# A four-level Perceiver block: reordering inside the last cross attention, and turned logits in the soft mixture of experts

## The chip, the cores and the metric

The kernel runs on one core of one Trainium2 chip. The metric is the device time of one execution in microseconds (us), taken as the median of several executions. The engines are TensorE (PE: matrix products and transposes, its weight loads shown apart as PEld), VectorE (DVE), ScalarE (ACT), GpSimd (POOL) and the queue of the SyncE engine (SP), from which every transfer of this kernel is issued. All arithmetic around the change is in float32.

## The reference

The kernel computes twelve residual layers on `x` (2 batches, 128 tokens, width 256); a cross attention reads a context of 2048 tokens per batch. The change touches two of the twelve.

The soft mixture of experts of level 1 (16 experts, 128 slots each, hidden width 64):

```python
x_n = _l2norm(x_ln, -1) * scale
mu_n = _l2norm(mu, 0)
logits = jnp.einsum('bnd,des->bnes', x_n, mu_n)
dispatch = jax.nn.softmax(logits, axis=1)                            # over the 128 tokens
combine = jax.nn.softmax(logits.reshape(B, N, E * S), axis=-1)       # over the 2048 slots
slot_in = jnp.einsum('bnd,bnes->besd', x_ln, dispatch)
h = jax.nn.gelu(jnp.einsum('besd,edh->besh', slot_in, W1) + b1[None, :, None, :], approximate=False)
slot_out = jnp.einsum('besh,ehd->besd', h, W2) + b2[None, :, None, :]
out = jnp.einsum('bsd,bns->bnd', slot_out.reshape(B, E * S, D), combine)
```

The cross attention of level 3 (16 query heads of width 128, 4 key/value heads; the keys are the context and the 128 tokens themselves, 17 tiles of 128):

```python
q = _rope(_rms_norm((x @ Wq.T)...)); k = _rope(_rms_norm((kv_in @ Wk.T)...)); v = kv_in @ Wv.T
scores = jnp.einsum('bhqd,bhkd->bhqk', q, k) * SCALE
probs = jax.nn.softmax(scores, axis=-1)
attn = jnp.einsum('bhqk,bhkd->bhqd', probs, v)
return attn.transpose(...).reshape(...) @ Wo.T
```

## The kernel before

Each layer is a block: a hand-written program for each engine, tied by semaphores, with a barrier of all engines at its end. Order within an engine is the order in which the block's function issues. PSUM has eight banks of 128x512 float32.

**Soft mixture of experts (`l1_ffn`, L1217 to L1526).** `xst` is the normalised `x`, turned, `xlt` the layer-normed one, `k.mu` the slot matrix 256x2048, `k.mu_row` the reciprocal norms of its columns spread over all partitions, `k.mu_col` the same reciprocals laid down the partitions, one column per expert (made in `l1_attn`, L1141 to L1169). The logits are made twice:
- `combine_logits(n)` (L1289; its matmuls are recorded at the helper's L212): tokens on the partitions, 512 slots at a time, eight pieces, into banks 4, 5, 2 in turn (`PIECE_BANK`); `take_logits(n)` on DVE multiplies by `k.mu_row` into `comb` (L1465) and takes the maximum (L1467); `combine_exps(b)` on ACT (L1411) exponentiates all 2048 in place.
- `dispatch_logits(p)` (L1304, also recorded at L212), for each of eight pairs of experts: slots on the partitions, eight 128x256 matmuls into bank 0. `dispatch_max(p)` on DVE (L1476, L1477) finds the maximum over tokens, `exps(p)` on ACT (L1406) exponentiates with `k.mu_col` as scale.

Behind that, for each pair: `dispatch_norm` (DVE L1482, L1484), `turn` (PE L1320), `take_turned` (DVE L1490), `hidden` (PE L1344), `gelu` (ACT L1422), `slot_out` (PE L1355), `add_bias` (DVE L1505); `turn_combine` (PE L1332) turns the pair's part of `comb`, `take_combine` (DVE L1496) copies it, `combine` (PE L1363) adds up the output in banks 6 and 7. The pairs are software pipelined: iteration i issues on PE, in this order, `dispatch_logits(i)`, `turn(i-1)`, `turn_combine(i-3)`, `hidden(i-2)`, `slot_out(i-3)`, `combine(i-4)` (L1370). On ACT, iteration i is `exps(i)` and `gelu(i-2)`, which need different function tables, so that a table is loaded before each. `first_product(n)` (four pieces of `x_ln @ W1`, copied out by `take_product(n)` on ACT, L1416) and the eight `combine_logits` lie inside iterations 0 and 1.

**Cross attention (`l3_xattn`, L2196 to L2738).** The work is in eight units u (batch x key/value head, four query heads each). `loop(u)` in this text is the loop over the 17 key tiles j at L2484: PE issues `values(u, j)` (L2416, weighs the values with the exponentials of tile j), `scores(u+1, j)` (L2389), and at some j a `project(u+2, i)` (L212) or a `turn_group(u+2, i)` (L2379). A tile of 128x512 weights, `wt(j)`, lives through: scores in one of three PSUM banks; `copy_scores` (ACT L2557); `maxima` (DVE L2674, the first is a copy, L2671); later `shifts` (DVE L2684, subtracts the row's maximum), `exps` (ACT L2567), `values` (PE). `copy_scores(u+1, j)` waits until `values(u, j)` has read the tile. Between two loops stands `between(u)` on each engine: PE turns the maxima (`turn_max`, L2396, waits for the last `maxima`), spreads them (`spread_max`, L2402), and, for u of 2 and more, makes five value pieces (`project_values`, L212 with `x_wv`; units 0 and 1 make one, their others come from earlier layers), which ACT copies (`take_values`, L2542); `turn_out(u-1)` (L2425, copied by ACT at L2574) and `project_out(u-1)` (L212) finish the unit before.

How far the shifts and the exponentials run ahead of the loop:

```python
AHEAD_SHIFT, AHEAD_EXP = 3, 2                       # L2245
for j in range(AHEAD_SHIFT): shifts(u, j)           # DVE, L2719, then in the loop:
    if j + AHEAD_SHIFT < KT3: shifts(u, j + AHEAD_SHIFT)
    if u + 1 < NU: maxima(u + 1, j)
    if j + AHEAD_EXP < KT3: exps(u, j + AHEAD_EXP)  # ACT, L2622
    if u + 1 < NU: copy_scores(u + 1, j)
```

DVE has extra work in two loops: `angle_step` (L2151 to L2165) at j of 8 and more in loop(0), `table_step` (L2178 to L2185) at j of 12 and more in loop(1), and ACT has `sines` (L2193) ahead of loop(1). POOL finishes the projected keys and queries (L2505 to L2514).

## Time and profile before

| | us |
|---|---|
| median of 3 runs (range) | 1604.55 (1602.79 to 1605.17) |
| the profiled execution's own time | 1604.83 |
| span of its profile | 1603.1 |
| PE busy | 1413.8 (88%) |
| DVE busy | 1122.8 (70%) |
| ACT busy | 868.8 (54%) |
| POOL busy | 469.7 (29%) |

The profile records one execution. Its span runs from the first to the last instruction; the 1.7 us up to that execution's own time lie around it. A busy share is an average over all twelve layers; what a change is worth is read in its own layer. "PEclk" is TensorE's granted clock as a share of 2.4 GHz, so 0.50 is 1.2 GHz.

### The profile page before, as it was taken

The numbers are of one execution on the slowest core, as the hardware profiler recorded it, in microseconds if no ns is written. First come the engines' busy times: TensorE is split into PE (matmuls) and PEld (weight loads), VectorE is DVE, ScalarE is ACT, GpSimd is POOL, SyncE is SP. The second block draws the span as 40 slices with busy tenths as digits, with TensorE's granted clock in tenths as the row PEclk, the third lists the DMA queues.
The fourth block names the chain that finished last, engine by engine and source line by source line (L and its number), as shares of the span: only waits on it lengthen the run. The fifth ranks groups of instructions, "written<-read, shape, count | busy, mean of one in ns | idle before, by whom it ended". The sixth has DMA issues, their size and how long they took to land. (4 is left out here: it accounts for less than half of the span.)

```text
span 1603.1 us, 23976 instructions
## 1 busy us (share of the span) xinstructions
PE 1413.8 (88%) x8072; PEld 993.9 (62%) x8072; DVE 1122.8 (70%) x2240; ACT 868.8 (54%) x2300; POOL 469.7 (29%) x515
## 2 busy tenths in 40 slices
PE   7876988867998789987779899999998989999969
PEld 5653444445775457876557677877777436666657
DVE  4687999825665555764559768766854679999953
ACT  2446989832124264426445445445554579999831
POOL 2244000000000001530447326534600037777710
PEclk9986999977999799998889899999999999999979
DMA  3002999965341402200200000000000453333120
GB/s 144 1 1 51 180 185 186 178 183 162 105 136 33 99 14 51 90 1 1 79 2 12 14 8 8 14 1 1 1 1 10 141 159 119 101 103 114 40 78 8
DMA packets 192390, 112.89 MB, mean 70 GB/s; under 512 B 150233, under 2 KB 166617, under 8 KB 191628
## 3 DMA queue, kind: packets, MB, share of 16 engines
q1 hardware_dynamic: 192268, 111.35, 26.7%
q8 instruction: 65, 1.06, 0.3%
q14 instruction: 57, 0.47, 0.1%
HBM read 77.51 MB, written 0.26 MB: 49 GB/s over the span
## 5 line engine op out<-in xcount | busy, mean ns | idle before, releaser
L672 DVE TENSOR_REDUCE x_row_max<-banks 128x1 f32<-128x512 f32 x248 | 152.7, 682 | 14.4 <-PE banks L366 14.3
L575 ACT ACTIVATE x_v_full<-banks,x_neg_max,x_q_scale 128x1024 int16<-128x1024 f32 x128 | 153.4, 1202 | 15.1 <-DMA x_v_full<-x_v_full 7.6
L212 PE MATMUL banks<-a_w_ring,x_normed_T 128*128 128x512 f32 x320 | 146.6, 598 | 4.8 <-DVE a_r L3193 4.8
L2389 PE MATMUL banks<-ctx_tokens,x_kT 128*128 128x512 f32 x272 | 139.8, 601 | 2.4 <-ACT ctx_tokens L2551 2.4
L2416 PEld LDWEIGHTS banks<-x_v,x_weights_T 128*128 128x128 f32 x896 | 111.2, 193 | 30.0 <-ACT x_weights_T L2567 15.9
L2416 PE MATMUL banks<-x_v,x_weights_T 128*128 128x129 f32 x896 | 118.8, 278 | 7.8 <-ACT x_weights_T L2567 7.8
L2505 POOL TENSOR_TENSOR ctx_tokens<-ctx_tokens 128x512 f32<-128x512 f32 (+1 forms) x48 | 71.4, 1487 | 136.6 <-DVE ctx_tokens L2655 136.6
L2674 DVE TENSOR_TENSOR ctx_tokens<-ctx_tokens,x_weights_T 128x512 f32<-128x512 f32 x104 | 88.3, 849 | 31.7 <-ACT x_weights_T L2557 31.2
L366 PE MATMUL banks<-x_kT_parts,x_qT_int 64*128 64x512 bf16 x512 | 103.5, 402 | 7.1 <-DVE x_row_max L672 3.5
L2684 DVE TENSOR_TENSOR x_weights_T<-x_weights_T,ctx_tokens 128x512 f32<-128x512 f32 x112 | 90.2, 829 | 24.8 <-ACT ctx_tokens L2563 24.7
L427 PEld LDWEIGHTS banks<-x_v_full,x_v_int 128*16 128x16 f16 x1024 | 57.2, 91 | 76.3 <-DMA x_v_full<-x_v_full 46.4
L212 PEld LDWEIGHTS banks<-a_w_ring,x_normed_T 128*128 128x128 f32 x320 | 59.1, 192 | 68.8 <-issue 68.8
L3083 POOL TENSOR_TENSOR a_rms<-a_rms,a_minus_half 128x4 f32<-128x4 f32 x64 | 64.9, 1014 | 116.4 <-ACT a_rms L3013 116.4
L427 PE MATMUL banks<-x_v_full,x_v_int 128*16 128x128 f16 x1024 | 81.2, 224 | 18.8 <-DMA x_v_full<-x_v_full 18.1
L2526 ACT ACTIVATE ctx_tokens<-banks 128x512 f32<-128x512 f32 (+1 forms) x48 | 26.1, 543 | 124.1 <-DVE ctx_tokens L2655 124.1
L3090 POOL TENSOR_TENSOR a_r<-a_r 128x256 f32<-128x256 f32 x128 | 89.7, 732 | 4.7 <-DVE a_r L3193 4.7
L2557 ACT COPY x_weights_T<-banks 128x512 f32<-128x512 f32 x112 | 64.9, 586 | 22.5 <-PE banks L2389 22.5
L3008 ACT ACTIVATE a_junk<-banks 128x128 bf16<-128x128 f32 x256 | 67.1, 276 | 17.4 <-PE banks L212 15.7
L3174 DVE SCALAR_TENSOR_TENSOR banks<-banks,a_rms,a_norm_w 128x128 f32<-128x128 f32 x256 | 69.2, 347 | 6.2 <-POOL a_rms L3083 6.0
L333 PE MATMUL banks<-x_wkv,ctx_T 128*128 128x256 f32 x256 | 72.4, 431 | 0.0
L212 PEld LDWEIGHTS banks<-x_wk,ctx_T 128*128 128x128 f32 x512 | 61.4, 192 | 17.6 <-issue 13.4
L886 POOL TENSOR_SCALAR mask_bias<-mask 128x2048 f32<-128x2048 uint8 x2 | 3.8, 1902 | 230.5 <-POOLq L186 230.4
(532 smaller groups left out, 3374.4 us busy)
## 6 DMA issues: line engine op xcount, KB each, us to landing
a_w_ring<-in_L_attn_WB_T SPq DMA_DIRECT2D x16, 512.0 KB
a_w_ring<-in_L_attn_WC_T SPq DMA_DIRECT2D x16, 512.0 KB
f_w_gate_up<-in_L_ffn_gate_up SPq DMA_DIRECT2D x18, 352.0 KB
ctx_tokens<-in_ctx SPq DMA_DIRECT2D x16, 256.0 KB, 5.7
x_wq<-in_L_xattn_Wq_T SPq DMA_DIRECT2D x8, 512.0 KB, 3.7
a_w_ring<-in_L_attn_Wth_T SPq DMA_DIRECT2D x8, 512.0 KB
a_bias_ring<-in_L_attn_B_bias_perm SPq DMA_DIRECT2D x16, 256.0 KB
a_bias_ring<-in_L_attn_C_bias_perm SPq DMA_DIRECT2D x16, 256.0 KB
```

Source lines behind the costliest of these rows:

```text
L212: last = nc.tensor.matmul(out, lhsT, rhs, start=(i == 0), stop=(i == len(pairs) - 1))
L333: last = nc.tensor.matmul(k.bank(bank, P, D, i * D), k.ctxt[:, c, a:a + P], wkv[:, c, half * D:(half + 1) * D], start=False, stop=(i == 1 ...
L366: return nc.tensor.matmul(k.bank(bank), qt[lo:lo + 64, h // 2, b * T:(b + 1) * T], kt[lo:lo + 64, h // 2, a:a + 512], start=True, stop=True)
L427: last = nc.tensor.matmul(k.ps[lane:lane + HD, 6, 0:P], vq[:, tile, h * HD:(h + 1) * HD], pt16[:, q % RING, i], start=(tile == 0), stop=(t ...
L575: nc.scalar.activation(eb[:, q % RING], k.ps[:, 2 + 2 * (q % 2):4 + 2 * (q % 2), :].rearrange("p a n -> p (a n)"), ACT.Exp, bias=nb[:, v % ...
L672: nc.vector.reduce_max(mx[:, u % 2, i:i + 1], k.bank(MBANK[m % 3]), AX.X).then_inc(s.max_taken, 1)
L2389: nc.tensor.matmul(k.bank(s_bank(key)), kt[:, u % 2, j * P:(j + 1) * P], flat(qt[:, u % 2]), start=True, stop=True).then_inc(s.scores_in_p ...
L2416: last = nc.tensor.matmul(k.bank(O_BANKS[h // 2], P, HD3 + 1, (h % 2) * (HD3 + 1)), wt(j)[:, h * P:(h + 1) * P], vt[:, u % 2, j], start=Fa ...
L2505: nc.gpsimd.tensor_tensor(t1[:, r, 0:w], t1[:, r, 0:w], t2[:, m % 2, 0:w], ALU.add).then_inc(s.turned, 1)
L2674: nc.vector.tensor_tensor(flat(top), flat(top), wt(j), ALU.max).then_inc(s.maxed, 1)
L2684: nc.vector.tensor_tensor(wt(j), wt(j), flat(shift), ALU.subtract).then_inc(s.shifted, 1)
L3090: last = nc.gpsimd.tensor_tensor(a, a, r2[:, j, :, 1 - hf], op)
```

## The change

In `l3_xattn`:
- the shifts start eight tiles ahead of the weighing instead of three, the exponentials four instead of two;
- on PE, `between(u)` issues its last three value pieces together, then the two zeroing matmuls that open the output banks (now `open_values(u)`, formerly at the head of `values(u, 0)`), then `project_out(u-1)`; before, `project_out(u-1)` stood ahead of the fifth piece and the zeroing matmuls came last. The wait for the copied values stays at the head of `values(u, 0)`;
- on ACT, `between(u)` issues exponentials 0 to 3 with the copies of the value pieces between them.

In `l1_ffn`:
- `dispatch_logits(p)` is gone. `turn_logits(p)` transposes the pair's four 128x128 blocks of `comb`, which holds the finished logits, into bank 0. The exponentials of the combine softmax go to another tile (`cexp`, in the place of `k.mu`), so that `comb` stays;
- the scale by `k.mu_col` falls away in `exps(p)`, and `k.mu_col` with the four transposes, the copy and the semaphore that made it in `l1_attn`;
- `combine_logits` goes by slots first and batch second; four pieces come ahead of the pair loop, two each in iterations 0 and 1; `first_product` and `take_product` come two each in iterations 1 and 2; both `combine_exps` come in iteration 2, behind the last two `take_product` and ahead of the first `gelu`.

```diff
@@ l1_attn @@
-                pe.wait_ge(s.kk_ready, 1)
-                for q4 in range(4):
-                    last = nc.tensor.transpose(k.bank(1, P, P, q4 * P), k.mu_norm[:, q4 * P:(q4 + 1) * P], k.ident[:])
-                last.then_inc(s.col_in_psum, 1)
...
-                act.wait_ge(s.col_in_psum, 1)
-                nc.scalar.copy(k.mu_col[:].rearrange("p (j q) -> p q j", j=4), k.bank(1).rearrange("p (q j r) -> p q j r", q=4, j=4)[:, :, :, 0]).then_inc(k.mu_ready, 1)
@@ l1_ffn @@
-        ncol = sb("neg_mu_rnorm", [P, ne])
+        cexp = k.mu[:].rearrange("p c s -> p (c s)").rearrange("p (b s) -> p b s", b=B)
...
                 def combine_logits(n):
-                    b, j = divmod(n, 4)
+                    j, b = divmod(n, B)
+                    if b == 0 and j == 0:
+                        pe.wait_ge(s.xT_ready, B)
...
-                def dispatch_logits(p):
-                    if p == 0:
-                        pe.wait_ge(s.xT_ready, B)
-                    else:
+                def turn_logits(p):
+                    pe.wait_ge(s.logits_taken, B * (p // 2 + 1))
+                    if p >= 1:
                         pe.wait_ge(s.dexp_ready, 4 * p)
                     for e in range(2):
                         a = (2 * p + e) * SLOTS
-                        last = matmul_acc(nc, k.bank(0, P, BT, e * BT), [(k.mu[:, c, a:a + SLOTS], xst[:, c]) for c in range(DC)])
+                        for b in range(B):
+                            last = nc.tensor.transpose(k.bank(0, P, P, (e * B + b) * T), comb[:, b, a:a + SLOTS], k.ident[:])
                     last.then_inc(s.dlog_ready, 1)
...
+                for n in range(4):
+                    combine_logits(n)
+                steps = ((0, turn_logits), (1, turn), (3, turn_combine), (2, hidden), (3, slot_out), (4, combine))
...
-                        if lag == 1 and i < 2:
-                            for n in range(4 * i, 4 * i + 4):
+                        if lag == 0 and i < 2:
+                            for n in range(4 + 2 * i, 6 + 2 * i):
                                 combine_logits(n)
-                        if lag == 1 and i == 1:
-                            for n in range(4):
+                        if lag == 1 and i in (1, 2):
+                            for n in range(2 * i - 2, 2 * i):
                                 first_product(n)
...
-                act.wait_ge(k.mu_ready, 1)
...
                     if i in (1, 2):
-                        combine_exps(i - 1)
-                    if i == 1:
-                        for n in range(4):
+                        for n in range(2 * i - 2, 2 * i):
                             take_product(n)
+                    if i == 2:
+                        for b in range(B):
+                            combine_exps(b)
                     if i >= 2:
                         gelu(i - 2)
...
+                for n in range(4):
+                    take_logits(n)
                 for i in range(NPAIR + 3):
                     if i < NPAIR:
                         dispatch_max(i)
                     if 0 <= i - 1 < NPAIR:
                         take_turned(i - 1)
                     if i < 2:
-                        for n in range(4 * i, 4 * i + 4):
+                        for n in range(4 + 2 * i, 6 + 2 * i):
                             take_logits(n)
@@ l3_xattn @@
-        AHEAD_SHIFT, AHEAD_EXP = 3, 2
+        AHEAD_SHIFT, AHEAD_EXP = 8, 4
...
                 def values(u, j):
                     if j == 0:
                         pe.wait_ge(s.v_taken, values_before(u + 1))
-                        if u:
-                            pe.wait_ge(s.on_ready, u)
-                        else:
-                            pe.wait_ge(s.filled, 3)
-                        for bank in O_BANKS:
-                            nc.tensor.matmul(k.bank(bank, P, 2 * (HD3 + 1)), zero[:, 0:P], zero[:], start=True, stop=False)
...
+                def open_values(u):
+                    if u:
+                        pe.wait_ge(s.on_ready, u)
+                    else:
+                        pe.wait_ge(s.filled, 3)
+                    for bank in O_BANKS:
+                        nc.tensor.matmul(k.bank(bank, P, 2 * (HD3 + 1)), zero[:, 0:P], zero[:], start=True, stop=False)
...
-                    if v:
-                        project_values(u, v.pop(0))
+                    while v:
                         project_values(u, v.pop(0))
+                    open_values(u)
                     if u:
                         project_out(u - 1)
-                    if v:
-                        project_values(u, v.pop(0))
...
-                    exps(u, 0)
-                    if v:
-                        take_values(u, v.pop(0))
-                        exps(u, 1)
-                        take_values(u, v.pop(0))
-                        take_values(u, v.pop(0))
-                    else:
-                        exps(u, 1)
+                    for j in range(AHEAD_EXP):
+                        exps(u, j)
+                        if v:
+                            take_values(u, v.pop(0))
```

## Rows read from the trace of the kernel before

**Rows 1.** Windows over the two layers (busy us, instructions).

```profile
542.70:629.70 87.00, 76.62 (x376) 51.87 (x376) 50.64 (x105) 44.63 (x104) 0.00 (x0) 0.94 0.27 64
789.40:1238.00 448.60, 420.36 (x2640) 328.99 (x2640) 307.08 (x499) 216.03 (x412) 181.75 (x168) 0.96 0.02 7
```

**Rows 2.** Timeline of PE, one pair of experts, iteration 6 (start, us, what).

```profile
602.21 1.89 PE L212 MATMUL banks<-f_x_l_T,mu 128*128 128x256 f32 x8
603.93 0.60 PE L1320 MATMUL banks<-ident,f_disp 128*128 128x128 f32 x4
604.37 0.60 PE L1332 MATMUL banks<-ident,f_combine 128*128 128x128 f32 x4
...
608.40 1.89 PE L212 MATMUL banks<-f_x_l_T,mu 128*128 128x256 f32 x8
```

**Rows 3.** Timeline of ACT and DVE, pairs 3 to 7 of the experts.

```profile
587.81 0.46 ACT L1406 ACTIVATE f_disp<-banks,f_disp_small,mu_rnorm_cols 128x128 f32<-128x128 f32 x1
...
589.69 1.28 ACT L1422 ACT_TABLE_LOAD   x1
...
592.77 0.46 ACT L1406 ACTIVATE f_disp<-banks,f_disp_small,mu_rnorm_cols 128x128 f32<-128x128 f32 x1
...
600.77 0.18 DVE L1482 RECIPROCAL f_disp_small<-f_disp_small 128x4 f32<-128x4 f32 x1 [0.73 <-ACT f_disp L1406]
...
611.25 0.46 ACT L1406 ACTIVATE f_disp<-banks,f_disp_small,mu_rnorm_cols 128x128 f32<-128x128 f32 x1 [1.23 <-DVE f_disp_small L1477]
```

**Rows 4.** The tile `comb`: its DVE and ACT instructions (ns min/median/max).

```profile
L1465 DVE TENSOR_TENSOR f_combine<-banks,mu_squares x8: 692/692/692, 556.0 to 571.3; 128x512 f32<-128x512 f32 x8
...
L1411 ACT ACTIVATE f_combine<-f_combine,f_small x2: 2002/2004/2006, 566.3 to 582.6; 128x2048 f32<-128x2048 f32 x2
```

**Rows 5.** Timeline of PE, start of the experts' layer.

```profile
549.48 3.78 PE L212 MATMUL banks<-f_x_l_T,mu 128*128 128x256 f32 x8 [0.46 <-ACT f_x_l_T L1393]
...
564.27 7.03 PE L212 MATMUL banks<-mu,f_x_l_T 128*128 128x512 f32 x16
```

**Rows 6.** Windows: busy us of PE, PEld, DVE, ACT, POOL; then PEclk.

```profile
550.00:555.00 5.00, 5.00 (x11) 3.28 (x10) 0.85 (x2) 0.74 (x1) 0.00 (x0) 0.50 1.16 193
580.00:582.00 2.00, 0.93 (x12) 0.52 (x9) 1.39 (x3) 1.14 (x5) 0.00 (x0) 1.00 0.00 0
832.40:885.90 53.50, 44.73 (x264) 33.09 (x263) 45.99 (x67) 25.15 (x49) 28.48 (x24) 0.94 0.03 10
886.00:888.00 2.00, 1.76 (x8) 1.47 (x8) 1.82 (x5) 0.20 (x1) 0.00 (x0) 0.54 0.00 0
896.00:898.00 2.00, 2.00 (x12) 1.47 (x11) 0.00 (x0) 1.97 (x3) 0.00 (x0) 0.90 0.04 8
944.00:946.00 2.00, 2.00 (x10) 2.00 (x11) 1.79 (x6) 0.00 (x0) 0.00 (x0) 0.54 0.00 0
```

**Rows 7.** Timeline of PE, its waits in the cross attention.

```profile
873.06 1.16 PE L2416 MATMUL banks<-x_v,x_weights_T 128*128 128x129 f32 x8 [1.77 <-ACT x_weights_T L2567]
...
885.94 0.97 PE L2396 MATMUL banks<-ident,ctx_tokens 128*128 128x128 f32 x4 [3.32 <-DVE ctx_tokens L2674]
...
943.98 0.97 PE L2396 MATMUL banks<-ident,ctx_tokens 128*128 128x128 f32 x4 [2.17 <-DVE ctx_tokens L2674]
...
990.85 1.16 PE L2416 MATMUL banks<-x_v,x_weights_T 128*128 128x129 f32 x8 [0.70 <-ACT x_weights_T L2567]
...
1214.83 0.61 PE L212 MATMUL banks<-x_wv,x_normed_T 128*128 128x128 f32 x4
1215.80 0.39 PE L2413 MATMUL banks<-x_zero 1*128 1x258 bf16 x2 [0.36 <-ACT x_v L2542]
```

**Rows 8.** Timeline of DVE in loop(0) of the cross attention.

```profile
832.45 2.50 DVE L2684 TENSOR_TENSOR x_weights_T<-x_weights_T,ctx_tokens 128x512 f32<-128x512 f32 x4 [5.19 <-ACT ctx_tokens L2563]
839.03 0.43 DVE L2671 COPY ctx_tokens<-x_weights_T 128x512 f32<-128x512 f32 x1 [4.08 <-ACT x_weights_T L2557]
...
866.92 1.64 DVE L2684 TENSOR_TENSOR x_weights_T<-x_weights_T,ctx_tokens 128x512 f32<-128x512 f32 x1
```

More of the change, by code:

```diff
@@ L1114, in l1_attn @@
         with signals(nc, k.pool, "dve_step xt_ready proj_ready low_ready exp_ready dec_ready scanned den_in_psum den_ready o_ready out_ready "
-                     "select_ready row_in_psum row_taken col_in_psum kk_ready") as s, nc.Block() as block:
+                     "select_ready row_in_psum row_taken kk_ready") as s, nc.Block() as block:
             @block.sync
@@ L1331, in turn_combine @@
                         for b in range(B):
-                            last = nc.tensor.transpose(k.bank(2, P, P, (e * B + b) * T), comb[:, b, a:a + SLOTS], k.ident[:])
+                            last = nc.tensor.transpose(k.bank(2, P, P, (e * B + b) * T), cexp[:, b, a:a + SLOTS], k.ident[:])
                     last.then_inc(s.ct_in_psum, 1)
@@ L1369, in _ @@
                     turn_x(b)
-                steps = ((0, dispatch_logits), (1, turn), (3, turn_combine), (2, hidden), (3, slot_out), (4, combine))
+                for n in range(4):
+                    combine_logits(n)
+                steps = ((0, turn_logits), (1, turn), (3, turn_combine), (2, hidden), (3, slot_out), (4, combine))
                 for i in range(NPAIR + 4):
@@ L1406, in exps @@
                             nc.scalar.activation(disp[:, r, e, b], k.bank(0, P, T, (e * B + b) * T), ACT.Exp, bias=dm[:, r, 1, e, b:b + 1],
-                                                 scale=k.mu_col[:, 2 * p + e:2 * p + e + 1], accum_out=dm[:, r, 2, e, b:b + 1]).then_inc(s.dexp_ready, 1)
+                                                 accum_out=dm[:, r, 2, e, b:b + 1]).then_inc(s.dexp_ready, 1)
                 def combine_exps(b):
                     act.wait_ge(s.cmax_ready, b + 1)
-                    nc.scalar.activation(comb[:, b], comb[:, b], ACT.Exp, bias=sm[:, b, 4:5], accum_out=sm[:, b, 5:6]).then_inc(s.cexp_ready, 1)
+                    nc.scalar.activation(cexp[:, b], comb[:, b], ACT.Exp, bias=sm[:, b, 4:5], accum_out=sm[:, b, 5:6]).then_inc(s.cexp_ready, 1)
                 def take_product(n):
@@ L1452, in _ @@
                                                    op0=ALU.mult, op1=ALU.add).then_inc(s.xl_ready, 1)
-                dve.wait_ge(k.mu_ready, 1)
-                nc.vector.tensor_scalar(ncol[:], k.mu_col[:], -1.0, None, ALU.mult)
                 for b in range(B):
@@ L1461, in take_logits @@
                 def take_logits(n):
-                    b, j = divmod(n, 4)
+                    j, b = divmod(n, B)
                     sl = slice(j * 512, (j + 1) * 512)
@@ L1469, in take_logits @@
                         link(last)
+                        if b == 0:
+                            dve.wait_ge(s.logits_ready, 8)
                         link(nc.vector.reduce_max(sm[:, b, 10:11], mx4[:, b], AX.X))
@@ L1476, in dispatch_max @@
                     link(nc.vector.tensor_reduce(dm[:, r, 0], k.bank(0).rearrange("p (e b t) -> p e b t", e=2, b=B), AX.X, ALU.max))
-                    nc.vector.tensor_tensor(dm[:, r, 1], dm[:, r, 0], ncol[:, 2 * p:2 * p + 2].unsqueeze(2).to_broadcast([P, 2, B]), ALU.mult).then_inc(s.dmax_ready, 1)
+                    nc.vector.tensor_scalar(dm[:, r, 1], dm[:, r, 0], -1.0, None, ALU.mult).then_inc(s.dmax_ready, 1)
                 def dispatch_norm(p):
@@ L3422, in build @@
                 k.xscale = k.sb("x_scale", [P, 1], F32, to_f1)
-                k.mu_col = k.sb("mu_rnorm_cols", [P, EXPERTS], F32, to_f1)
                 k.musq = k.sb("mu_squares", [P, DC, EXPERTS * SLOTS], F32, to_f1)
```

1 line of the change is left out of this document (removed).

## The prediction

> **What bounds the kernel now.** The busy shares say TensorE, but the change touches two layers, so I read windows over these two first. The experts' layer takes 87.0 us, of which PE is busy 76.6; the cross attention from its first scores on takes 448.6, PE busy 420.4 [rows 1]. Both are bound by PE most of the time, and PE is idle 10 and 28 us. A gain can come from less PE work or from these idle times; whatever ends sooner is passed on whole, since each layer closes with a barrier and nearly no transfers run there (DMA share 0.02 in the second [rows 1]).
>
> Then I read the timelines. In the experts' pair loop, what to see is the distance between two `dispatch_logits`: 6.19 us (602.21 to 608.40), PE without a gap [rows 2]. ACT's own distance, where PE is not yet in the way, is 4.96 (587.81 to 592.77), two table loads of 1.28 included [rows 3]. In the cross attention, what to see is where PE waits: for an exponential inside the loops (1.77, 0.70), for the last maximum ahead of `turn_max` (3.32 and 2.17), and for the last value copy (0.36) [rows 7].
>
> **Experts, the pair loop.** Per pair eight matmuls go, 1.72 us of PE (602.21 to 603.93), and four transposes come, 0.44 by the same shape next to them (603.93 to 604.37) [rows 2]: 6.19 - 1.72 + 0.44 = 4.91. Next in line are ACT with 4.96 and a chain through DVE: the exponentials take 1.88 (587.81 to 589.69 [rows 3]), then DVE runs reciprocal, normalisation, two bias additions and the maximum, four operations near 0.69 [rows 4] and small ones near 0.2 [rows 3], together 5.0 to 5.1. Three limits within 0.2 us of each other rarely mesh perfectly; I take 5.1 (bounds 4.96 and 5.3, the latter if PE waits 0.4 for the normalised tile that the long matmuls used to hide). From `exps(3)` to `exps(7)` it took 611.25 - 587.81 = 23.4 [rows 3]; four times 5.1 is 20.4: **3.0 gained** (2.2 to 3.6). The tail behind `exps(7)` has the same work.
>
> A rule of the Trainium skill speaks against this. "ScalarE: Activation LUTs", section "What ACT_TABLE_LOAD costs", gives 1.28 us for a load plus a drain of 1.38 at every switch. By it ACT would need about 7.7 per pair and the gain would be nil. The trace has two switches in 4.96 us, so here the drain costs nothing more.
>
> **Experts, the start.** Now the PE queue runs: pieces 0 to 3, turned logits 0, pieces 4, 5, turned logits 1, pieces 6, 7, `turn(0)`, products 0, 1, turned logits 2, `turn(1)`, products 2, 3. It starts at 549.48 as before [rows 5]. At full clock a piece takes 1.7 (7.03 for four, the end hidden by the next [rows 5]); the clock is 1.2 GHz until about 555 [rows 6], so those 5.5 us do the work of 2.75 and piece 3 ends at 559.1. DVE takes pieces at 1.4 each (two operations of 0.69 [rows 4]), done 560.7; maximum and sign 0.9, so 561.6; `exps(0)` 1.9, 563.5. I let its table load be done by then, since a single wait is left in front of it; otherwise 1.28 more. PE has ended piece 5 at 563.0, turns logits 1 until 564.0, and pieces 6, 7 until 567.5. `turn(0)` ends 568.0, products 0, 1 and logits 2 at 571.8. On DVE, `take_turned(0)` now stands ahead of the last two pieces: 568.9, two pieces with their final maxima 3.7, 572.6, normalisation 573.5. PE idles 1.8 for it, then `turn(1)` and products 2, 3 end at 577.5. ACT copies until 578.3, then the two combine exponentials, each 2.0 plus a read-out of the sum [rows 4], until 582.5; table load, gelu 0.47, table load: `exps(3)` at 585.5 against 587.81: **2.3 gained** (1.0 to 2.5). The eight small operations that made `k.mu_col` lay beside DVE's longer work: nothing. The first product starts at 568.0 instead of 571; its weights were asked for when the layer began, 25 us before, and I take no wait for them.
>
> **Cross attention, loops.** After the first shifts DVE has nothing to do: 4 shifts take 2.50, then 4.08 idle until the first scores of the next unit are copied [rows 8]. Five more shifts (5 x 0.6 = 3.0) fit there, in every unit, and five are gone from j = 9 to 13. ACT's two more exponentials (0.53 each by start distance) fall in a wait of the same kind. The slack between a shift and the exponential that needs it grows from one tile to four, so the waits for exponentials go.
> - loops 2 to 5 each have one of 0.70 [rows 7]: 4 x 0.7 = **2.8**. In loops 6 and 7 I found none.
> - loop(0): DVE sets `turn_max` at 885.94 [rows 7]. Of the 53.5 us before, it is busy 46.0 [rows 6], and more than half of the idle rest is the 4.08 at the start; late in the loop it is full. Without five shifts, one of which takes 1.64 (866.92 [rows 8]), it ends 3.0 to 3.6 sooner. PE's scattered waits of 3.5 (1.77 is the longest) move to the end, in front of `turn_max`. **3.4**.
> - loop(1): DVE's extra work comes late, from j = 12. Until then, as I read its timeline, its maxima wait for ACT's copies, so that a removed shift shows as idle time; only about three count, and the sines start two exponentials later, 0.3 behind. **1.5** (1.0 to 3.0).
>
> The shift of 1.64 is a 0.6 us operation held up by a POOL operation. "SBUF — State Buffer", section "Who interferes with whom", has it that a DVE instruction with two SBUF inputs is blocked for the whole of a GpSimd instruction that reads SBUF. The trace agrees with that in size. By it the lock passes to the next maximum and loop(0) gains 3.0; without it 3.6 or more.
>
> **Cross attention, between.** For units 2 to 7, from the fifth value piece (1214.83) to the zeroing matmuls (1215.80) PE spends 0.97 [rows 7], of which the piece needs 0.44 (as four 128x128 [rows 2]). `project_out` now stands there, 1.7 us, which covers the copy: 6 x 0.5 = **3.0** (2.2 if part of the wait returns at `values(u, 0)`).
>
> **Sum.** 3.0 + 2.3 + 2.8 + 3.4 + 1.5 + 3.0 = 16.0. From the profiled execution's own 1604.83 that is 1588.8, and as it lies 0.3 above the median of 1604.55, **1588.5**. With all low ends (2.2, 1.0, 2.8, 3.0, 1.0, 2.2 = 12.2) 1592.3; with all high ones (3.6, 2.5, 2.8, 3.6, 3.0, 3.0 = 18.5) 1586.0.
>
> **Rivals.**
> - *The clock falls in the experts' layer (2 in 10).* PE now idles 1.8 us at 571.8, 2.6 from 579.9 to 582.5 (for the combine exponentials) and 2.1 ahead of logits 4. Before, idle waits of 1.9 near 581 left the clock at 1.00 [rows 6], while 2.17 and 3.32 in the cross attention were followed by 0.54 [rows 6, 7]. At 1.2 GHz a pair's 4.9 us of PE become 9.8; one pair or a little less is paid until the clock is back: 3 to 5 us, so **1592.5**. "TensorE: Matmul & The Clock Gate", section "HAM oscillation — how this bites in real kernels", also has gaps of idle PE bring the clock down; the trace agrees at 886 and 944.
> - *The clock stays up at a unit's change (1.5 in 10).* At 944 PE's idle 2.17 stays near 2.0 by my count (its loop waits of 1.3 join it, 1.5 go), so I leave it; if it doesn't fall, the transposes and values there (0.97 for four instead of 0.60 [rows 2, 7]) save 1.7, and at 886 up to 4.4: 1582.5 to 1587, **1585**.
> - *One layer only (0.5 in 10).* The limits of the pair loop mesh badly, or PE's first idle times eat the start: the experts give nothing, **1594**.
> - *The change's waits do not go (0.2 in 10).* If the 0.7 waits came from something else than the shifts' slack, and DVE's end is set by its copies alone, under 3 us: **1602**. Against it: the row names ACT, behind a DVE that never pauses.
> - *Slower (0.3 in 10).* The clock falls at 580 and, since the loop at 9.8 per pair never idles but short transposes now make up a third of it, stays down for the rest. Five pairs cost 5 x 4.9 = 24.5: **1613**. It decides from three and a half slow pairs on (16 / 4.9). Against it: at 886, with a clock just fallen and further pauses of PE behind it, it was at 0.90 again from 896 on [rows 6], 10 us or two pairs later.
>
> **The numbers.** My forecast has 5.5 in 10, its own range 1585.5 to 1592.5. With the two clock cases and room for sizes that I read, 8 in 10 lie in 1582 to 1597. A measurement of this kernel tells about 0.2% (3.2 us) from no change. Faster 0.94, within 0.03, slower 0.03.
>
> **What the profile after would show.** `exps` of consecutive pairs 5.0 to 5.2 apart and `exps(3)` some 2.3 sooner relative to the layer's first piece; no waits for L2567 on PE in loops 2 to 5; `turn_max(1)` still waiting, for about 3.5 us, but 3.4 sooner relative to the loop's start; no wait at L2413 for an x_v copy. Wrong I would be by a PE clock of 0.5 within the pair loop, by a wait of DVE or ACT between pairs that adds over 0.4, or by DVE in loops 0 and 1 pausing for copies as much as it lost in shifts.

## The result, and the profile after

The changed kernel takes 1587.69 us (median of 4 runs, 1583.83 to 1592.33) against 1604.46 for the kernel before (4 runs, 1602.79 to 1605.17): a ratio of 0.9898, 95% interval 0.9868 to 0.9928, or 16.8 us less (the ratio is worked out over all runs and is not the quotient of the two medians). Timed once more, it took 1588.20 against 1605.46: 0.9891 (0.987 to 0.9911). The profiled execution took 1589.59, its span is 1587.3 us.

To see where the time went, I measure two stretches of each trace by the start of the same work: **A**, the experts' layer from the first matmul of its logits (dispatch logits before, combine logits after) to the end of the last combine, and **B**, the cross attention from the first `turn_max` to the start of the last `turn_out`.

| us | before | after | gain |
|---|---|---|---|
| A, first piece to the fourth pair's exponentials | 38.33 | 35.07 | 3.26 |
| A, from there to the eighth pair's exponentials | 23.44 | 19.51 | 3.93 |
| A in all | 79.03 | 71.84 | 7.19 |
| B, unit 1 | 60.53 | 57.47 | 3.06 |
| B, unit 2 | 58.04 | 56.85 | 1.19 |
| B, units 3 to 6 | 56.31, 54.63, 54.62, 54.63 | 54.92, 53.23, 53.22, 53.23 | 5.59 |
| B, unit 7 and the last | 41.81, 26.66 | 41.38, 26.23 | 0.86 |
| B in all | 407.23 | 396.53 | 10.70 |
| all else in the span | 1116.8 | 1118.9 | -2.1 |

("First piece" is the first matmul of the logits. A row of B is the distance from one `turn_max` to the next; unit 1 ends at `turn_max(1)`.)

Windows over the two layers of the changed kernel; the rows of before are [rows 1]:

```profile
549.60:637.00 87.40, 79.81 (x399) 54.45 (x398) 51.83 (x107) 44.14 (x105) 4.15 (x6) 0.92 0.31 71
819.60:1270.00 450.40, 430.85 (x2620) 331.91 (x2621) 309.51 (x518) 229.20 (x426) 155.45 (x151) 0.96 0.06 19
```

They don't cover the same work as [rows 1]: they begin 6 and 36 us later in their layers and run on into the layers behind, so that the busy times can't be set against each other. They say little about who sets the pace, and the timelines say more. PE in the experts' loop, two pairs apart by 4.90 us (598.51 to 603.41), without a gap; before it was 6.19 [rows 2]:

```profile
598.51 0.60 PE L1306 MATMUL banks<-ident,f_combine 128*128 128x128 f32 x4
598.95 0.60 PE L1315 MATMUL banks<-ident,f_disp 128*128 128x128 f32 x4
599.39 0.60 PE L1327 MATMUL banks<-ident,mu 128*128 128x128 f32 x4
...
603.41 0.60 PE L1306 MATMUL banks<-ident,f_combine 128*128 128x128 f32 x4
```

ACT in the same loop, the first exponential of pairs 3, 4, 5, 6 and 7, counted from 0 (against [rows 3]):

```profile
585.47 0.37 ACT L1402 ACTIVATE f_disp<-banks,f_disp_small 128x128 f32<-128x128 f32 x1
...
586.99 1.28 ACT L1418 ACT_TABLE_LOAD   x1
...
590.07 0.37 ACT L1402 ACTIVATE f_disp<-banks,f_disp_small 128x128 f32<-128x128 f32 x1
...
595.18 0.37 ACT L1402 ACTIVATE f_disp<-banks,f_disp_small 128x128 f32<-128x128 f32 x1 [0.52 <-DVE f_disp_small L1474]
...
600.08 0.37 ACT L1402 ACTIVATE f_disp<-banks,f_disp_small 128x128 f32<-128x128 f32 x1 [0.31 <-DVE f_disp_small L1474]
...
604.98 0.37 ACT L1402 ACTIVATE f_disp<-banks,f_disp_small 128x128 f32<-128x128 f32 x1 [0.31 <-DVE f_disp_small L1474]
```

Two things weren't foreseen. An exponential takes 0.37 us, not 0.46, so ACT's own distance is 4.60 (585.47 to 590.07) and no longer 4.96. And from pair 5 on ACT waits, 0.52 and then 0.31 each: pairs go by PE's 4.90. Why PE is behind is in its waits and in the clock. Its two longest waits just ahead of these pairs:

```profile
582.43 0.65 PE L1327 MATMUL banks<-ident,mu 128*128 128x128 f32 x4 [2.20 <-ACT mu L1407]
584.30 1.13 PE L1339 MATMUL banks<-f_disp_tok,mu_squares 128*64 128x128 f32 x8 [1.22 <-ACT f_hT L1418]
```

The windows behind them, and those at the changes to units 2 and 3 (the last three numbers are granted clock, DMA share, GB/s):

```profile
582.00:584.00 2.00, 0.65 (x4) 0.42 (x4) 0.69 (x1) 1.97 (x4) 0.00 (x0) 0.80 0.00 0
584.00:586.00 2.00, 1.70 (x12) 1.32 (x14) 0.00 (x0) 1.97 (x5) 0.00 (x0) 0.50 0.00 0
586.00:590.00 4.00, 4.00 (x20) 3.07 (x16) 2.92 (x7) 3.95 (x9) 0.00 (x0) 0.50 0.04 13
590.00:592.00 2.00, 2.00 (x18) 1.35 (x18) 1.46 (x4) 1.97 (x10) 0.00 (x0) 0.99 0.47 117
...
877.00:879.00 2.00, 1.83 (x8) 1.67 (x8) 1.82 (x6) 0.00 (x0) 0.00 (x0) 0.50 0.00 0
879.00:887.00 8.00, 7.43 (x25) 5.80 (x25) 5.21 (x9) 5.34 (x9) 0.00 (x0) 0.50 0.00 1
887.00:889.00 2.00, 2.00 (x11) 1.32 (x11) 0.76 (x2) 1.98 (x3) 0.00 (x0) 1.00 0.00 0
936.00:938.00 2.00, 2.00 (x11) 2.00 (x11) 0.00 (x0) 0.10 (x1) 0.00 (x0) 0.50 0.00 0
938.00:940.00 2.00, 2.00 (x19) 2.00 (x18) 0.37 (x1) 1.47 (x3) 0.00 (x0) 0.95 0.00 0
```

In these windows the clock is at 1.2 GHz at three places: for some 7 us in the experts' layer, where before it was 1.00 [rows 6], and at the changes to units 2 and 3, as before. (It is at 0.50 for another 14 us from the first `turn_max` on, behind a wait of 4.3 us, in every trace here, so that no comparison turns on it.)

In the cross attention PE still waits for the last maximum at units 1 and 2, 3.87 and 2.49 us (3.32 and 2.17 before [rows 7]):

```profile
877.16 1.11 PE L2395 MATMUL banks<-ident,ctx_tokens 128*128 128x128 f32 x4 [3.87 <-DVE ctx_tokens L2669]
...
934.01 0.66 PE L2395 MATMUL banks<-ident,ctx_tokens 128*128 128x128 f32 x4 [2.49 <-DVE ctx_tokens L2669]
...
1197.12 0.61 PE L211 MATMUL banks<-x_wv,x_normed_T 128*128 128x128 f32 x4
1197.66 0.39 PE L2419 MATMUL banks<-x_zero 1*128 1x258 bf16 x2
```

The last two lines answer to the last two of [rows 7]: the zeroing matmuls no longer wait. Now a window over a whole later unit, first of the kernel before (idle PE: 54.63 - 53.58 = 1.05 us):

```profile
998.61:1053.24 54.63, 53.58 (x359) 42.90 (x358) 38.61 (x63) 27.31 (x53) 25.76 (x24) 1.00 0.03 11
```

The same unit after, in which PE has no idle time left:

```profile
988.93:1042.16 53.23, 53.23 (x360) 42.98 (x359) 37.72 (x64) 27.20 (x53) 24.98 (x24) 1.00 0.04 11
```

DVE in loop(0), against [rows 8]: nine subtractions run in one go, and of the 4.08 us idle that they fill, 1.04 is left.

```profile
826.73 5.51 DVE L2679 TENSOR_TENSOR x_weights_T<-x_weights_T,ctx_tokens 128x512 f32<-128x512 f32 x9 [5.19 <-ACT ctx_tokens L2562]
833.27 0.43 DVE L2666 COPY ctx_tokens<-x_weights_T 128x512 f32<-128x512 f32 x1 [1.04 <-ACT x_weights_T L2556]
...
861.12 1.64 DVE L2669 TENSOR_TENSOR ctx_tokens<-ctx_tokens,x_weights_T 128x512 f32<-128x512 f32 x1
```

### The profile page after: what moved, and what is told of

It is laid out like the page before. It is cut to its first block and busy times, and to the rows that moved or that the text cites. A ratio compares the mean times of both kernels' runs of the same rounds, so it can differ in the third digit from the quotient of the medians.

```text
span 1587.3 us, 23902 instructions
## 1 busy us (share of the span) xinstructions
PE 1404.9 (89%) x8036; PEld 986.5 (62%) x8036; DVE 1116.5 (70%) x2239; ACT 864.6 (54%) x2299; POOL 465.4 (29%) x515
## 3 DMA queue, kind: packets, MB, share of 16 engines
q8 instruction: 64, 1.05, 0.3%
## 5 line engine op out<-in xcount | busy, mean ns | idle before, releaser
L574 ACT ACTIVATE x_v_full<-banks,x_neg_max,x_q_scale 128x1024 int16<-128x1024 f32 x128 | 153.3, 1202 | 16.8 <-DMA x_v_full<-x_v_full 8.9
L2679 DVE TENSOR_TENSOR x_weights_T<-x_weights_T,ctx_tokens 128x512 f32<-128x512 f32 x112 | 79.1, 757 | 24.7 <-ACT ctx_tokens L2562 24.7
```

The costliest lines, as they stand in the source:

```text
L574: nc.scalar.activation(eb[:, q % RING], k.ps[:, 2 + 2 * (q % 2):4 + 2 * (q % 2), :].rearrange("p a n -> p (a n)"), ACT.Exp, bias=nb[:, v % ...
L2679: nc.vector.tensor_tensor(wt(j), wt(j), flat(shift), ALU.subtract).then_inc(s.shifted, 1)
```

## The experiments

All numbers of them stand here once; A, B and "else" are read from each one's profiled execution. The first four rows ran beside the kernel before at 1604.88 us (median), the next four beside 1605.46, the last four beside 1603.75, and each ratio is against its own.

| kernel | median us | ratio (95%) | A | B | else |
|---|---|---|---|---|---|
| experts only | 1594.88 | 0.9944 (0.9928, 0.9961) | 71.77 | 405.88 | 1115.2 |
| cross attention only | 1594.16 | 0.9938 (0.9923, 0.9954) | 78.96 | 396.67 | 1117.1 |
| order only | 1601.44 | 0.998 (0.9968, 0.9993) | 78.94 | 403.48 | 1119.3 |
| subtractions only | 1595.13 | 0.9944 (0.9925, 0.9963) | 79.03 | 397.18 | 1117.6 |
| changed kernel again | 1588.20 | 0.9891 (0.987, 0.9911) | 71.89 | 396.53 | 1117.5 |
| pointer scale | 1589.42 | 0.9895 (0.9875, 0.9915) | 72.13 | 396.66 | 1116.8 |
| long fillers, cross | 1586.79 | 0.9881 (0.986, 0.9901) | 71.95 | 397.49 | 1115.6 |
| early combine exps | 1585.01 | 0.9869 (0.9848, 0.9889) | 68.83 | 396.52 | 1118.8 |
| fillers, experts | 1584.19 | 0.9879 (0.9861, 0.9898) | 70.68 | 396.48 | 1114.5 |
| short fillers, cross | 1584.11 | 0.9873 (0.986, 0.9887) | 71.74 | 393.95 | 1115.1 |
| early and fillers | 1582.14 | 0.9865 (0.9847, 0.9882) | 68.86 | 393.97 | 1117.5 |
| order of the start | 1605.00 | 1.0009 (0.9999, 1.0019) | 79.09 | 407.14 | 1116.6 |

The last column holds work that no kernel here touches, but for the few operations that made `k.mu_col`, and it runs from 1114.5 to 1119.3. So a median of few runs is good to some 2 us, while A repeats within 0.2 us and B, where the clock does the same, within 0.2: verdicts on one or two us rest on A and B.

**Each layer alone.** Experts only is the changed kernel with the cross attention of before; cross attention only is the reverse.

> Only the soft experts' half of the change. The two profiles put 7.2 us of the gain into that layer (first product of the logits to the end of the last weighted sum: 79.0 against 71.8), so my theory says 7 us faster than before, 1597.3, with the cross attention's marks at the old distances (60.5 and 58.0 from the first turning of the maxima to the second and third). The forecast's own sum says 5.3 us, 1599.2. A rival, that part of the layer's gain is given back by a colder clock in what follows, says 4 us or less, 1600.5.

> Only the cross attention's half. The profiles put 10.7 us into it, so 1593.8; distances between turnings of the maxima 57.5, 56.9, 54.9, 53.2, 53.2, 53.2, 41.4. If the two halves don't add up (a clock that depends on what came before), the time differs from 1593.8 by more than 2 us.

A gained 7.26 and 0.07, B 1.35 and 10.56: each layer's gain is its own. B's 1.35 in a kernel with the old cross attention is nearly all in unit 2 (58.04 to 56.77), where PE's clock was at 0.50 for some 3 us behind `turn_max(1)` in place of 10. The medians gained 10.0 and 10.7, 3 to 4 more in sum than the changed kernel's 16.8 and 17.3; A and B add up (7.26 + 10.56 = 17.8 against 17.9), so I put the rest down to unit 2 and to the last column; that is argued, not shown.

**The cross attention, split in two.** Order only moves the zeroing matmuls out of `values` into `open_values`, behind all value pieces, and `project_out` behind them:

```diff
-                    if v:
-                        project_values(u, v.pop(0))
-                        project_values(u, v.pop(0))
-                    if u:
-                        project_out(u - 1)
-                    if v:
-                        project_values(u, v.pop(0))
+                    while v:
+                        project_values(u, v.pop(0))
+                    open_values(u)
+                    if u:
+                        project_out(u - 1)
```

> In the cross attention only PE's new order between units (the value pieces together, the output banks opened, then the unit before projected); shifts and exponentials 3 and 2 ahead as before. Theory: the wait for the last value copy goes in six units, 0.43 us each, 2.6 us in all, 1601.9, and the 0.7 us waits for an exponential at j = 13 stay. Rival: the order needs the earlier exponentials, and the wait comes back at the first weighing: no change.

Subtractions only changes one number of the kernel before:

```diff
-        AHEAD_SHIFT, AHEAD_EXP = 3, 2
+        AHEAD_SHIFT, AHEAD_EXP = 8, 2
```

> In the cross attention only the shifts eight ahead; exponentials two ahead, old order between units. Theory: all of the loops' gain (3.1 in loop 0, 1.2 in loop 1, 0.96 in each of loops 2 to 5, 8.1 us in all, 1596.3) is the shifts', and the exponentials four ahead give nothing more. Rival: with exponentials still two ahead, ACT's order leaves waits of 0.3 to 0.7 us for them in loops 2 to 5, and no more than 5 us are gained, 1599.5.

A middle unit (before 54.63) is 54.20 with the order alone, 53.70 with the subtractions alone and 53.23 with both and the exponentials four ahead: 0.43 + 0.93 = 1.36 of 1.40. In such a unit the exponentials' lead adds at most 0.04. In unit 2 it costs: with the subtractions alone that unit is 56.29, in the changed kernel 56.85, with the clock at 0.50 for some 10 us in both. The two exponentials more stand ahead of ACT's sines, and ACT's first copy of scores comes 13.52 us behind `turn_max(1)` instead of 12.30. (The B of the order alone, 3.75 under the first, holds 1.2 of the clock: its unit 2 is 56.82, with the short fall of experts only.) PE's timeline with the order alone keeps the wait for an exponential in each unit:

```profile
989.82 1.16 PE L2410 MATMUL banks<-x_v,x_weights_T 128*128 128x129 f32 x8 [0.69 <-ACT x_weights_T L2567]
...
1044.01 1.16 PE L2410 MATMUL banks<-x_v,x_weights_T 128*128 128x129 f32 x8 [0.70 <-ACT x_weights_T L2567]
```

With the subtractions alone it keeps the wait for the value copy, and, shown above it, the one for the last maximum ahead of unit 3:

```profile
940.26 0.66 PE L2396 MATMUL banks<-ident,ctx_tokens 128*128 128x128 f32 x4 [2.44 <-DVE ctx_tokens L2674]
...
1003.84 0.39 PE L2413 MATMUL banks<-x_zero 1*128 1x258 bf16 x2 [0.36 <-ACT x_v L2542]
```

Each wait was worth more than its idle time: 0.69 of idle gave 0.93, 0.36 gave 0.43. The kernel before shows why, in the same loop with a wait and without:

```profile
1043.76 1.02 PE L2389 MATMUL banks<-ctx_tokens,x_kT 128*128 128x512 f32 x2
1045.48 1.16 PE L2416 MATMUL banks<-x_v,x_weights_T 128*128 128x129 f32 x8 [0.69 <-ACT x_weights_T L2567]
1046.47 1.02 PE L2389 MATMUL banks<-ctx_tokens,x_kT 128*128 128x512 f32 x2
...
1048.66 1.02 PE L2389 MATMUL banks<-ctx_tokens,x_kT 128*128 128x512 f32 x2
1049.52 1.05 PE L2416 MATMUL banks<-x_v,ctx_tokens 128*128 128x129 f32 x8
1050.41 1.02 PE L2389 MATMUL banks<-ctx_tokens,x_kT 128*128 128x512 f32 x2
```

Without a wait the next group starts 0.86 behind the start of the last one, though that one's row says 1.02: the two overlap. With the wait it starts 1.72 behind, 0.86 later, of which only 0.69 count as idle; and the group behind the wait takes 0.99 to the next start, not 0.89.

At 940.26 PE had stood for 2.44 us, and yet the clock stayed at 1.00 and unit 3 took 53.75. After 2.16 us idle at the same place in the experts-only kernel it fell to 0.50 and unit 3 took 56.32; of the 2.57 between them the subtractions explain 0.93, and 1.64 are left for the clock.

**The changed kernel again.**

> The changed kernel itself, timed once more. Its first times ran from 1583.8 to 1592.3 us, while the experts' half alone gained 10.0 and the loops' half alone 10.7. If the two gains add, this comes out near 1584 us, 20 us under the kernel before; if the first median was right, near 1588, and the two halves share a gain of some 3 us (a fall of the clock at a unit's change, which each of them escapes alone, is what they could share).

A 71.89 and B 396.53 repeat the first trace to 0.05 us, and the median came out near 1588, the rival's value. The rival's reason, a fall of the clock that each half escapes alone, is borne out in part: the clock falls at the same three places in both traces of the changed kernel, and in cross attention only at the same two of B, but in experts only the fall at the change to unit 2 was the short one, worth 1.3 us. (The kernel before had the long one in its trace.)

**What an exponential costs.**

```diff
-                                                 accum_out=dm[:, r, 2, e, b:b + 1])
+                                                 scale=k.ones[:, 0:1], accum_out=dm[:, r, 2, e, b:b + 1])
```

> The changed kernel, but its dispatch exponentials take their scale from a 128x1 operand again (a column of ones). Theory: that operand is what made an exponential 0.46 us instead of 0.37, so they come back to 0.46 and four of them give ScalarE 0.37 us more for each pair; ScalarE's chain of a pair goes from 4.60 to 4.97 us and becomes the bound instead of TensorE's 4.90, so the start of a pair's exponentials follows the last by 4.97 to 5.0 us, and the layer is longer by 4 x 0.07 + 0.37 for the pair that ScalarE set already + about 0.4 in the start: 1 us, 1588.6 if the changed kernel is at 1587.7. Rival: the duration is that of the logits' bank or of their placement, so nothing changes.

ACT's first exponential of two pairs:

```profile
594.34 0.46 ACT L1402 ACTIVATE f_disp<-banks,f_disp_small,ones 128x128 f32<-128x128 f32 x1
...
599.31 0.46 ACT L1402 ACTIVATE f_disp<-banks,f_disp_small,ones 128x128 f32<-128x128 f32 x1
```

With the operand back, an exponential is 0.46 again and the distance 4.97 (594.34 to 599.31), ACT without a wait. The duration is the operand's doing, as "ScalarE: Activation LUTs" of the Trainium skill has it (section "What ACT_TABLE_LOAD costs": some 93 ns for each such operand; the trace agrees, 0.09). The layer grew by 0.24 to 0.29 only: the fourth pair's exponentials start 35.40 us behind the first piece instead of 35.07, and behind them PE, which sets the layer's end with its 4.90 a pair, stands still for less than 0.1 more. My 1 us was too much, and the times can't tell it from nothing.

**Where the start's gain is from.** The kernel before with the changed order of pieces, products and combine exponentials, but with its dispatch logits still matmuls:

```diff
-                    b, j = divmod(n, 4)
+                    j, b = divmod(n, B)
...
-                        if lag == 1 and i < 2:
-                            for n in range(4 * i, 4 * i + 4):
+                        if lag == 0 and i < 2:
+                            for n in range(4 + 2 * i, 6 + 2 * i):
                                 combine_logits(n)
...
```

> The kernel before, but for the order of the experts' start: combine logits by piece and not by half of the rows, four of them ahead of the loop, two products in each of two steps, both combine exponentials behind the fourth product. The dispatch logits are matmuls as before (1.8 us a pair against 0.45 for the turns), in the loop over pairs too, so that the pairs stay at 5.86. Theory: the start of the fourth pair's exponentials, 35.07 us behind the first piece in the changed kernel against 38.33, is set by TensorE's work ahead of it, in which three pairs' dispatch matmuls make up 3 x 1.35 = 4 us: with these back the order alone gives nothing or costs up to 0.8 us (1604 to 1605). Rival: the order makes the gain, since it puts the two combine exponentials (2 us each) where ScalarE stood: 2 to 3 us faster (1602).

PE's timeline, four pieces and then the first dispatch logits:

```profile
549.30 9.78 PE L212 MATMUL banks<-mu,f_x_l_T 128*128 128x512 f32 x16 [0.46 <-ACT f_x_l_T L1397]
558.92 1.89 PE L212 MATMUL banks<-f_x_l_T,mu 128*128 128x256 f32 x8
```

The fourth pair's exponentials start 587.68 - 549.30 = 38.38 us behind the first piece, against 38.33 before. The order alone gives nothing. What the changed kernel has on top is three pairs' dispatch matmuls less ahead of the fourth product, 3 x (1.73 - 0.44) = 3.9 us of PE, which covers the 3.3 gained; that they are its cause is argued from this sum. One thing else differs: here ACT still waits for `k.mu_ready`, its first table load starts at 561.82 only, and PE waits 0.79 us for the first exponentials; in the changed kernel that load is done at 552.20. The turned logits without the new order weren't run, and couldn't be as they stand, since they need the combine logits first.

**What the clock's fall costs in the experts' layer.** Two matmuls that nobody reads, in PE's 2.20 us wait:

```diff
                     if p == 0:
+                        for _ in range(2):
+                            nc.tensor.matmul(k.bank(4), k.ident[:], w1[:, 0, 0:512], start=True, stop=True)
                         pe.wait_ge(s.cexp_ready, B)
```

> The changed kernel, with two matmuls of 128x512 that nobody reads (0.88 us each), into a free bank, in TensorE's 2.20 us wait ahead of the first turn of the combine weights. Where the clock is at 1.00 from 580 us on (as in the kernel with the early combine exponentials, whose pairs follow each other by 4.61 us), TensorE never falls behind; where it is at 0.50 for 6 us (the changed kernel), TensorE is behind and the later pairs go by its 4.90. Theory: the fall costs the 0.5 us ahead of the sixth pair's exponentials and 0.3 for each of two or three pairs behind it, 1.1 to 1.4 us, and the fillers give that back: 1587 if the changed kernel is at 1588.2. The forecast's rival put it at 3 to 5 us. Rival now: only the 0.5 us, since the last combine sets the end of the layer and not the exponentials.

A window over the stretch in which the clock had fallen:

```profile
580.00:590.00 10.00, 7.00 (x54) 5.01 (x54) 4.89 (x10) 9.86 (x25) 0.00 (x0) 1.00 0.10 28
```

ACT's first exponential of pairs 4, 5 and 6:

```profile
588.29 0.37 ACT L1404 ACTIVATE f_disp<-banks,f_disp_small 128x128 f32<-128x128 f32 x1
...
592.90 0.37 ACT L1404 ACTIVATE f_disp<-banks,f_disp_small 128x128 f32<-128x128 f32 x1
...
597.50 0.37 ACT L1404 ACTIVATE f_disp<-banks,f_disp_small 128x128 f32<-128x128 f32 x1
```

PE's timeline of the same kernel, the last two times that it stands still in this layer:

```profile
585.34 0.63 PE L1306 MATMUL banks<-ident,f_combine 128*128 128x128 f32 x4 [1.08 <-ACT f_disp L1404]
586.19 0.66 PE L1315 MATMUL banks<-ident,f_disp 128*128 128x128 f32 x4 [0.22 <-DVE f_disp L1483]
```

The clock is 1.00 throughout, the exponentials of pairs follow each other by 4.61, and A is 70.68: the fall cost 1.2 us, inside the 1.1 to 1.4 expected. But 4.61 is not the layer's pace. PE needs 4.90 a pair, runs without a gap from 586.19 to the last combine, and so sets the end of the layer here too; the exponentials keep 4.61 only because PE starts with a lead, which is used up at the last pair. In the changed kernel the half clock stretched PE's way from the second `hidden` matmuls to the third from 4.69 us (582.52 to 587.21 here) to 5.82 (584.30 to 590.12): 2.4 us more of work, of which 1.3 fell into the idle time shown above and 1.1 were left. The clock fell here in all six traces that have the changed experts' layer as it is, and in none of the three with the fillers or with the early combine exponentials below. The median went down by more (4 us, across two comparisons), but 3 of that stand in the last column.

**The clock at the changes of unit.** First with too many fillers:

```diff
                 def turn_max(u):
+                    if u in (1, 2):
+                        pe.wait_ge(s.shift_ready, u)
+                        if u >= 2:
+                            pe.wait_ge(s.out_taken, u - 1)
+                        for _ in range(8 if u == 1 else 5):
+                            nc.tensor.matmul(k.bank(M_BANK), k.ident[:], wv[:, 0, 0:512], start=True, stop=True)
```

> The changed kernel, with matmuls that nobody reads, into the maxima's bank, in TensorE's two waits for the last maxima of units 1 and 2 (8 and 5 of 128x512, 3.6 and 2.2 us of 3.87 and 2.49). Theory: the half clock in the 10 us behind the first wait and the 2 us behind the second comes from TensorE having stood still there; with the stretch filled the clock stays at 1.0, and as the third unit is 54.9 us where the clock fell at its start and 53.7 where it did not, and VectorE, not TensorE, sets the second, it gains 1.2 to 1.7 us. Rival 1: the fall belongs to the change of unit (other small matmuls with gaps), so it comes all the same: 0. Rival 2: the fillers themselves run late into the turn of the maxima: slower by up to 0.5.

I had misread the cost of a filler: the rows give 0.44 for each record, and a 128x512 matmul in f32 is two. The eight ran 7.0 us and delayed `turn_max(1)` by 2.9 (unit 1: 60.34); the clock stayed at 1.00 and unit 3 took 53.23. With `4 if u == 1 else 2` instead:

> The fillers in the waits for the last maxima again, 4 and 2 of 128x512 in place of 8 and 5: each took 0.88 us, not 0.44, so that the eight ran 7.0 us and held the turn of the maxima back by 2.9. 4 run 3.5 of the 3.87 us, 2 run 1.8 of the 2.49. Theory: clock at 1.00 at both changes of unit as with the long ones, third unit 53.2 instead of 54.9, fourth as it is, second unit 57.5 as it is: 1.7 us faster than the changed kernel, and 0.2 more in the second. Rival: the 0.4 to 0.7 us left over are enough for the clock to fall: 0.

PE's timeline, the fillers (two records each) and the turn of the maxima behind them:

```profile
871.09 3.60 PE L2396 MATMUL banks<-x_wv,ident 128*128 128x512 f32 x8
875.12 0.65 PE L2401 MATMUL banks<-ident,ctx_tokens 128*128 128x128 f32 x4 [0.43 <-DVE ctx_tokens L2675]
```

Windows where the clock had fallen:

```profile
877.00:887.00 10.00, 9.08 (x48) 6.54 (x49) 5.92 (x10) 8.02 (x10) 0.00 (x0) 1.00 0.05 15
932.00:940.00 8.00, 8.00 (x68) 7.59 (x67) 5.92 (x12) 4.99 (x10) 0.00 (x0) 1.00 0.01 2
```

Units 1 to 3: 57.47, 55.91, 53.28 against 57.47, 56.85, 54.92, and B is 2.6 us shorter. The 1.64 of unit 3 is the price of its fall. The 0.94 of unit 2 isn't the price of all of its fall: some 16 us behind `turn_max(1)` the clock was at 0.50 after all, for some 3 us (0.50 from 892 to 894, 1.00 again from 896 on). The fillers made a long fall into a short one.

**The combine exponentials earlier.** The first half's go ahead of the third pair's exponentials, where ACT stood for 1.72 us:

```diff
                 for i in range(NPAIR + 2):
+                    if i == 2:
+                        combine_exps(0)
                     if i < NPAIR:
                         exps(i)
...
                     if i == 2:
-                        for b in range(B):
-                            combine_exps(b)
+                        combine_exps(1)
```

> The changed kernel, with the combine exponentials of the first half of the rows (2.0 us) put ahead of ScalarE's exponentials of the third pair, where ScalarE stands for 1.72 us and their maximum is there since 571.1. Theory: ScalarE's chain from the second half's exponentials to the first GELU sets when the loop over pairs gets going, so GELU 0 and the fourth pair's exponentials start about 1.9 us earlier and the 2.2 us wait ahead of the turn of the combine weights goes: 1.9 us faster. Rival: the third pair's exponentials, now 0.4 us later, push the fourth product's copy and the first hidden matmul, and only 1.4 us are left; or the fourth pair's logits, turned by TensorE behind that hidden matmul, hold it: under 1 us.

PE's timeline, its wait for the combine exponentials:

```profile
581.34 0.66 PE L1327 MATMUL banks<-ident,mu 128*128 128x128 f32 x4 [0.21 <-ACT mu L1407]
```

PE's wait of 2.20 is 0.21. The fourth pair's exponentials start 584.39 - 551.20 = 33.19 behind the first piece, 1.88 sooner. A gained 3.0 and not 1.9: without the long wait the clock does not fall either, and that gives the other 1.1, as the fillers did.

**Both together.**

> The early combine exponentials (3.0 us less in the layer of experts) and the short fillers in the cross attention together. If the gains add: 3.0 + 1.7 to 1.9, 4.8 us faster than the changed kernel at 1588, 1583.3.

A 68.86 and B 393.97: 3.0 + 2.6 = 5.6 us less than the changed kernel, the gains add. The median is 1582.14 (1580.35 to 1584.58), 21.6 us under the kernel before of its comparison, where the changed kernel was 17.3 under its own. This version beats both kernels in A and B; the intervals of the two ratios (0.9847 to 0.9882 and 0.987 to 0.9911) still overlap a little.

## Why the prediction was right, step by step

It gave 1588.5, measured were 1587.7 and 1588.2. The sum of its terms was 16.0, the traces show 17.9 in A and B, and 2.1 of them are missing in the span because all else was longer in that execution. So part of the closeness is luck: the terms were low by 1.9. And two of the signs by which I would be wrong did show: a clock of 0.50 within the pair loop, and a wait of ACT of 0.52 between pairs. The exponentials of pairs came 4.60, 5.11, 4.90 and 4.90 apart, not 5.0 to 5.2. The other signs were right: no wait of PE for an exponential in loops 2 to 5, none for the value copy, and 3.87 us (for 3.5) ahead of `turn_max(1)`.

- **Pair loop, 3.0.** It measured 3.9. PE's 4.91 was right (4.90). The term was too small because I let three limits near 5.0 mesh into 5.1; ACT's was really 4.60, as the removed scale operand shortens each exponential by 0.09, and I had the row's operand list [rows 3] in front of me without pricing it. The DVE chain that I put at 5.0 to 5.1 is 4.44 in the changed kernel (585.47 to 589.91): the same four exponentials are shorter by 0.36, and operations of 0.69 start 0.6 apart. So the 3.9 are two things that I didn't have: with the clock up, exponentials 3 to 7 take 18.42 instead of 23.44, 5.0 less, and the fall took 1.1 back. The term came near by luck.
- **Start, 2.3.** It measured 3.3. `exps(3)` began at 585.47, where I had computed 585.5, but in this execution the first piece began at 550.40, not at 549.48, so the chain to it was 0.9 shorter than mine; that is already so where the combine exponentials start (27.9 us behind the first piece, 28.8 by my sum). Most of it is PE's wait for the normalised tile, 1.12 us where I had 1.8. The table load was done ahead, as I took it. The order alone gives none of it.
- **Loops 2 to 5, 2.8.** It measured about 3.9 (4 x 0.96). The waits were the ones named; what I mis-sized is their price. I took the idle time, but with both waits of a unit PE's busy time shrank as well, by 53.58 - 53.23 = 0.35: a wait takes away the overlap with the matmuls before it, and the first group behind it takes 0.1 longer.
- **loop(0), 3.4.** 3.06. The next maximum takes the 1.64 that a subtraction had (861.12), while POOL's operation on two tiles in SBUF runs from 859.89 to 862.21. That is the rule of "SBUF — State Buffer" of the Trainium skill, "Who interferes with whom": by it I had 3.0, and the trace agrees.
- **loop(1), 1.5.** 1.19 between these two traces, both with a clock of 0.50 for some 10 us. By the traces the subtractions gave 1.75 (58.04 to 56.29 with them alone) and the two exponentials ahead of the sines took 0.56 back, where I had 0.3. The clock moves this unit by as much: with the old subtractions it is 58.04 and 58.01 with the long fall, 56.77 and 56.82 with the short one.
- **Between, 3.0.** 6 x 0.43 = 2.6, by the order alone. I let the fifth piece need 0.44; it takes 0.54 to the next start (1197.12 to 1197.66).
- **The rival of the falling clock** (2 in 10) did happen: from 583 on the clock is at 0.50 for some 7 us. I had priced it at 3 to 5 us; it cost 1.2, because it slowed some 6 us of PE's work only, and 1.3 us of what that cost fell into time in which PE would have waited for ACT. The forecast and this rival were not exclusive, as I had made them. The slower case, in which the clock stays down in a loop of short transposes, did not come: it was back at 0.99 from 590 on.
- **The rival of the clock that stays up at a unit's change** did not occur in the change itself; filled, it is worth 2.6 us: 1.64 at unit 3, where I had 1.7, and 0.94 at unit 2, where I had up to 4.4 (and where a short fall stayed).

## What to carry to other kernels

Cost an operand that goes as well as an instruction that goes: a 128x1 scale on ScalarE is 0.09 us each time. When a change frees the bound engine, list the next three limits with their own rows; the lowest one may be hidden behind an engine that is only catching up. A wait ahead of a burst on TensorE costs its idle time, the overlap at its two ends, and perhaps the clock: if independent work can't be moved into it, matmuls that nobody reads are a cheap test of what the clock costs.

## What the runs showed of the hardware

- TensorE's clock is not a function of one wait: after 2.44 us idle it stayed at 1.00, after 2.16, 2.20 and 2.49 at comparable places it fell to 0.50. At the change to unit 2, behind 3.3 to 3.9 us, it fell in all eleven traces without fillers there, for some 3 us in two of them and some 10 in the others; the two lengths came with the same wait of 3.32.
- Two table switches in each pair never cost more than their 1.28 us loads: a pair of 4.60 us holds both.
- A 128x1 scale operand adds 0.09 us to a 128x128 exponential (0.46 against 0.37).
- A wait's removal gave 0.93 us for 0.69 idle and 0.43 for 0.36.
